# Attention and mixture-of-experts block on one Trainium2 core: the first scores in groups of four heads, POOL's normalisations as multiply and add, and unread matmuls ahead of the first scores

## The reference, cut to what matters

```python
def ref(x, ctx, lengths, ...):
    q = layernorm(x)                                   # (8, 128, 256): 8 heads of 16 channels, 256 queries
    s = 1 / (sqrt(64) * log(20)) * log(lengths)
    attn = softmax(s * einsum('bhdq,bhdk->bhqk', q, ctx))
    x = x + einsum('bhqk,bhdk->bhdq', attn, ctx)
    y = layernorm(x)
    # top-1 of eight experts with a capacity of 128 tokens each, plus a shared layer
    return x + gate * expert(y) + (silu(y @ sw1) * (y @ sw3)) @ sw2
```

## Time and profile before

| what | value |
|---|---|
| runs, median (lowest to highest) | 192.77 us (191.62 to 194.0), 3 runs |
| the profiled execution, its own time | 194.4 us |
| its span in the profile | 192.5 us |
| granted TensorE clock, mean | 0.949 |
| PE busy | 161.1 us (84%) |
| DVE, ACT, POOL busy | 104.3, 84.9, 70.9 us |

### The profile page before, as it was taken

One profiled execution on the slowest core, in us unless ns is written; L12 is line 12 of the kernel. 1 busy time (PEld: TensorE's weight loads), 2 busy tenths in 40 slices (PEclk: granted clock), 3 DMA queues, 4 the chain that ended last, 5 costly groups with the idle time before them and its releaser, 6 DMA issues.

```text
span 192.5 us, 3412 instructions
## 1 busy us (share of the span) xinstructions
PE 161.1 (84%) x1248; PEld 113.5 (59%) x1248; DVE 104.3 (54%) x236; ACT 84.9 (44%) x189; POOL 70.9 (37%) x79
## 2 busy tenths in 40 slices
PE   0399997999939999999999687299793999989960
PEld 0265566465425455555455387299692889878840
DVE  1466354556943778777341433422878228698630
ACT  2612122547453385665757363513761056455000
POOL 6644900691292081432202000044086047644241
PEclk9999999999985899999999999669999699999997
DMA  5999990000000000000070000002024935974001
GB/s 133 351 339 335 330 321 13 2 0 7 2 2 3 0 5 0 5 0 2 4 203 23 5 0 0 0 31 86 0 79 125 294 112 191 305 236 177 30 22 54
DMA packets 15697, 18.42 MB, mean 96 GB/s; under 512 B 1853, under 2 KB 14950, under 8 KB 15681
## 3 DMA queue, kind: packets, MB, share of 16 engines
q1 hardware_dynamic: 14240, 14.98, 25.3%
q0 software_dynamic: 1152, 2.97, 4.3%
q10 hardware_dynamic: 288, 0.26, 0.5%
HBM read 14.12 MB, written 4.21 MB: 95 GB/s over the span
## 4 chain that ended last, share of the span: by engine, by line
PE 70%; DVE 10%; DMA 5%; issue 5%; POOL 5%; ACT 2%; SPq 1%; DVEq 0%; POOLq 0%; ACTq 0%
PE bank L895 18%; PE bank L930 8%; PE bank L916 8%; PE bank L1049 5%; PE bank L977 5%; PE bank L979 4%; PE bank L1119 4%; DMA qz<-mrow 4%; POOL qz L352 3%; PE bank L1093 3%; PE bank L1094 3%; PE bank L942 2%; PE bank L957 2%; DMA leni<-in_lens 2%; PE bank L873 2%
## 5 line engine op out<-in xcount | busy, mean ns | idle before, releaser
L895 PE MATMUL bank<-kz,qz 32*128 32x256 f32 x256 | 50.2, 501 | 7.9 <-POOL qz L352 7.9
L487 DVE TENSOR_REDUCE nm<-bank 128x2 f32<-128x512 f32 x64 | 41.3, 686 | 26.7 <-PE bank L895 26.6
L916 PE MATMUL bank<-qz,kz 32*128 32x256 f32 x256 | 44.3, 442 | 1.1 <-DMA qz<-mrow 1.1
L733 ACT ACTIVATE pt<-bank 128x512 f32<-128x512 f32 x64 | 34.6, 590 | 23.1 <-PE bank L916 23.0
L895 PEld LDWEIGHTS bank<-kz,qz 32*128 32x128 f32 x256 | 31.2, 235 | 22.4 <-issue 16.1
L916 PEld LDWEIGHTS bank<-qz,kz 32*128 32x128 f32 x256 | 27.1, 205 | 6.5 <-issue 3.0
L352 POOL TENSOR_SCALAR qz<-xs,mv,rs 128x256 f32<-128x256 f32 x14 | 17.3, 1248 | 27.6 <-DVE rs L456 27.6
L930 PE MATMUL bank<-pt,vext 128*32 128x256 f32 x256 | 21.6, 413 | 0.0
L411 POOL DMA_INDIRECT expert_rows<-rk,idx_s x8 | 8.1, 1011 | 33.3 <-DVE rk L573 31.4
L377 POOL TENSOR_SCALAR rk<-xs,mv,rstd 128x256 f32<-128x256 f32 x6 | 7.4, 1225 | 31.9 <-ACT rstd L745 31.9
L434 POOL DMA_INDIRECT out<-vext,rk x8 | 8.3, 1037 | 13.1 <-DVE vext L652 9.1
(11 more groups left out here) (136 smaller groups left out, 302.4 us busy)
## 6 DMA issues: line engine op xcount, KB each, us to landing
wraw<-in_w SPq DMA_DIRECT2D x16, 352.0 KB, 7.2
wraw<-in_w SPq DMA_DIRECT2D x8, 256.0 KB, 7.1
expert_rows<-zero SPq DMA_DIRECT2D x1, 1032.0 KB, 10.3
out<-xs SPq DMA_DIRECT2D x8, 128.0 KB, 3.8
xs<-in_x SPq DMA_DIRECT2D x3, 256.0 KB, 4.3
cs<-in_ctx SPq DMA_DIRECT2D x3, 256.0 KB, 6.1
wraw<-in_w SPq DMA_DIRECT2D x8, 96.0 KB, 8.2
wraw<-in_sw SPq DMA_DIRECT2D x2, 352.0 KB, 5.6
```

The costliest lines, as they stand in the source:

```text
L487: nc.vector.tensor_reduce(nm[:, b % 2, :, place], mx_bank[n % NS][:].rearrange("p (u c) -> p u c", u=2), AX_X, ALU.max, negate=True).then_ ...
L733: nc.scalar.activation(pt[:, g % NPT, n % 4, :], sc_bank[n % NS][:], ACT.Exp).then_inc(exped, 1)
L895: mm = nc.tensor.matmul(mx_bank[n % NS][:, u * D:(u + 1) * D], qz[rows, b, half, u * P:(u + 1) * P], kz[rows, b, half, :], start=True, sto ...
L916: mm = nc.tensor.matmul(sc_bank[n % NS][:, c * D:(c + 1) * D], kz[rows, b, half, c * P:(c + 1) * P], qz[rows, b, half, :], start=True, sto ...
```

## The change

First scores: turns 0, 2, 4 and 6 issue the first scores of four heads (the last of two) at once, the first half of all four, then the second half. The first twelve heads (`FIRST`) go round six banks, head n waiting for the maximum of head n-6; the first three shifted scores wait for the maxima of heads 9, 10 and 11, whose banks they take. The transposed context now goes through bank 6 alone, one example at a time, in turns 1 to 8. POOL's queries become x * scale + (-mean * scale) with one more small DVE operation per chunk (`mrs`), POOL's token normalisation becomes x * rstd - (mean * rstd) with one more POOL operation on 128x1 (`mrs2`). PE's list begins with 50 rounds of four matmuls (bf16 ones, 32 rows by 128 columns, one in each row tile, into banks 0 to 3), which nobody reads.

```diff
+FIRST = 12
+IDLE_TURNS = 50
...
-VALUES = [min(b, LAG - 1) for b in range(B)]
+VALUES = [b + 1 for b in range(B)]
...
+            nc.gpsimd.memset(onesb[:], 1.0).then_inc(ones_set, 1)
             nc.gpsimd.memset(vext[:, :, :, :, HD:], 1.0).then_inc(ones_set, 1)
-            nc.gpsimd.memset(onesb[:], 1.0).then_inc(ones_set, 1)
...
-                pool.wait_ge(q_rs, chunk_of[b] + 1)
-                nc.gpsimd.tensor_scalar(qz[:, b, half, :], xs[:, b, :], mv[:, b, 0:1], rs[:, b, half:half + 1],
-                                        ALU.subtract, ALU.mult).then_inc(q_made, 1)
+                pool.wait_ge(q_shift, chunk_of[b] + 1)
+                nc.gpsimd.tensor_scalar(qz[:, b, half, :], xs[:, b, :], rs[:, b, half:half + 1],
+                                        mrs[:, b, half:half + 1], ALU.mult, ALU.add).then_inc(q_made, 1)
...
-                nc.gpsimd.tensor_scalar(x2[:, b, 0:D], xs[:, b, :], mv2[:, b, 0:1], rstd2[:, b:b + 1],
-                                        ALU.subtract, ALU.mult).then_inc(x2_made, 1)
+                nc.gpsimd.tensor_tensor(mrs2[:, b:b + 1], mv2[:, b, 0:1], rstd2[:, b:b + 1],
+                                        ALU.mult).then_inc(x_shift, 1)
+                pool.wait_ge(x_shift, b + 1)
+                nc.gpsimd.tensor_scalar(x2[:, b, 0:D], xs[:, b, :], rstd2[:, b:b + 1], mrs2[:, b:b + 1],
+                                        ALU.mult, ALU.subtract).then_inc(x2_made, 1)
...
+                dve.wait_ge(q_rs, i + 1)
+                nc.vector.scalar_tensor_tensor(mrs[:, a:z, :], mv[:, a:z, 0:1].broadcast_to(wide), -1.0,
+                                               rs[:, a:z, :], ALU.mult, ALU.mult).then_inc(q_shift, 1)
...
+                scores_bank = bank[n % (2 * NS) if n < FIRST else n % NS]
...
-                               sc_bank[b % NS][:, 0:2 * P].rearrange("p (c h d) -> p c h d", c=2,
+                               O[:, 0:2 * P].rearrange("p (c h d) -> p c h d", c=2,
...
+            def idle_turn(r):
+
+                nc.tensor.matmul(bank[r][:, 0:P], onesb[ROWS * r:ROWS * r + ROWS, :], onesb[ROWS * r:ROWS * r + ROWS, :],
+                                 start=True, stop=True)
+
+            pe.wait_ge(ones_set, 1)
+            for _ in range(IDLE_TURNS):
+                for r in range(4):
+                    idle_turn(r)
             pe.wait_ge(ld_cst, 16)
...
-                if b >= NS:
-                    pe.wait_ge(v_copied, b - NS + 1)
+                if b >= 1:
+                    pe.wait_ge(v_copied, b)
...
-                if n >= NS and u == 0:
-                    pe.wait_ge(maxed, n - NS + 1)
+                if n >= 2 * NS and u == 0:
+                    pe.wait_ge(maxed, n - 2 * NS + 1 if n < FIRST + NS else n - NS + 1)
...
-                if n == 0 and c == 0:
-                    pe.wait_ge(v_copied, B)
+                if n < NS and c == 0:
+                    pe.wait_ge(maxed, FIRST - NS + n + 1)
...
+                if m == 0:
+                    pe.wait_ge(v_copied, B)
...
+                if t < LAG and t % 2 == 0:
+                    heads = range(2 * t, min(2 * t + 4, 2 * LAG))
+                    for u in range(2):
+                        for n in heads:
+                            scores(n, u)
                 for part in range(2):
                     for k in range(2):
-                        if t < TURNS:
+                        if LAG <= t < TURNS:
                             scores(2 * t + k, part)
```

More of the change, by code:

```diff
@@ L163, in block_kernel @@
         rs = sb("rs", [P, B, 2], F32)
+        mrs = sb("mrs", [P, B, 2], F32)
         leni = sb("leni", [P, B], I32)
@@ L177, in block_kernel @@
         rstd2 = sb("rstd2", [P, B], F32)
+        mrs2 = sb("mrs2", [P, B], F32)
         x2 = rk
@@ L239, in block_kernel @@
         k_eager, k_made, q_eager, q_made = (sem(s) for s in ("k_eager", "k_made", "q_eager", "q_made"))
-        q_stats, q_mv, q_ln, q_rstd, q_rs = (sem(s) for s in ("q_stats", "q_mv", "q_ln", "q_rstd", "q_rs"))
+        q_stats, q_mv, q_ln, q_rstd, q_rs, q_shift = (
+            sem(s) for s in ("q_stats", "q_mv", "q_ln", "q_rstd", "q_rs", "q_shift"))
         v_turned, v_copied = sem("v_turned"), sem("v_copied")
@@ L246, in block_kernel @@
             sem(s) for s in ("o_copied", "o_turned", "inverted", "scaled", "o_back", "added"))
-        x_stats, x_mv, x_ln, x_rstd, x2_made = (sem(s) for s in ("x_stats", "x_mv", "x_ln", "x_rstd", "x2_made"))
+        x_stats, x_mv, x_ln, x_rstd, x_shift, x2_made = (
+            sem(s) for s in ("x_stats", "x_mv", "x_ln", "x_rstd", "x_shift", "x2_made"))
         x_turned, x_hi, x_lo = sem("x_turned"), sem("x_hi"), sem("x_lo")
@@ L486, in maximum @@
                 place = 4 * (h % 2) + h // 2
-                nc.vector.tensor_reduce(nm[:, b % 2, :, place], mx_bank[n % NS][:].rearrange("p (u c) -> p u c", u=2),
+                scores_bank = bank[n % (2 * NS) if n < FIRST else n % NS]
+                nc.vector.tensor_reduce(nm[:, b % 2, :, place], scores_bank[:].rearrange("p (u c) -> p u c", u=2),
                                         AX_X, ALU.max, negate=True).then_inc(maxed, 1)
@@ L710, in values @@
                 if b == 0:
-                    act.wait_ge(ones_set, 1)
+                    act.wait_ge(ones_set, 2)
                 nc.scalar.copy(vext[:, b, :, :, 0:HD],
-                               sc_bank[b % NS][:, 0:2 * P].rearrange("p (c h d) -> p c h d", c=2,
+                               O[:, 0:2 * P].rearrange("p (c h d) -> p c h d", c=2,
                                                                      h=H)).then_inc(v_copied, 1)
@@ L869, in turn_values @@
                 pe.wait_ge(ld_ctx[chunk_of[b]], 16)
-                if b >= NS:
-                    pe.wait_ge(v_copied, b - NS + 1)
+                if b >= 1:
+                    pe.wait_ge(v_copied, b)
                 for c in range(2):
-                    mm = nc.tensor.transpose(sc_bank[b % NS][:, c * P:(c + 1) * P], cs[:, b, c * P:(c + 1) * P], ident)
+                    mm = nc.tensor.transpose(O[:, c * P:(c + 1) * P], cs[:, b, c * P:(c + 1) * P], ident)
                 mm.then_inc(v_turned, 1)
@@ L892, in scores @@
                         pe.wait_ge(q_made, 2 * (b + 1) - EAGER)
-                if n >= NS and u == 0:
-                    pe.wait_ge(maxed, n - NS + 1)
-                mm = nc.tensor.matmul(mx_bank[n % NS][:, u * D:(u + 1) * D], qz[rows, b, half, u * P:(u + 1) * P],
+                if n >= 2 * NS and u == 0:
+                    pe.wait_ge(maxed, n - 2 * NS + 1 if n < FIRST + NS else n - NS + 1)
+                mm = nc.tensor.matmul(scores_bank[:, u * D:(u + 1) * D], qz[rows, b, half, u * P:(u + 1) * P],
                                       kz[rows, b, half, :], start=True, stop=True)
```

## The result

| | before | after |
|---|---|---|
| median of 20 runs each (lowest to highest) | 193.8 us (191.62 to 195.22) | 194.97 us (193.03 to 199.01) |
| ratio after / before, 95% interval | | 1.0097 (1.0065 to 1.0129) |
| the profiled execution: time, span | 194.4, 192.5 us | 194.63, 192.7 us |

The kernel became slower, by 1.2 us in the medians and by 1.9 us in the ratio, where 3.2 us of gain were forecast. It lies outside the stated range. The two profiled executions differ by 0.2 us only, because the one of before was 0.6 us slower than the median of its 20 runs.

A forecast was written before the change was run, and what follows sets the result against it. PE, busy 84% of the span, was taken as the bound, with waits on the maxima's transfer and POOL. Span: 192.5 + 0 + 2.2 - 5.4 = 189.3 us; from the median, -3.2 gives 189.6 us, range 186.2 to 193.4.

The forecast's parts named there:

- the moved values: Turns 7 to 9: transposes and ACT copies of examples 6 and 7 delay exponentials, +2.2 us, bounds 0 and 4.0.
- the clock behind 30 us: PE expected slow again after the pause, as before: gain and loss 0, bounds -1 and +1.5 us.
- rival (C): Clock rises later in turns 7 to 9 (+1.5), or the 57 us dip was not ordinary: 191.5 us, chance 0.18.
- Rival B: Moved values cost nothing, since exponentials have slack in turns 8 to 10: 187.4 us, chance 0.14.
- The transfer: Maxima's DMA before turn 7 stays behind weights and zeroing, landing unchanged at 30.0 us: gain 0, bounds 0 and 1.2.
- Rival A: The maxima's transfer follows its earlier issue, 1.2 to 4.8 us more gain, 3 taken: 186.6 us, chance 0.12.
- POOL: Around 51.6 us: multiply-and-add cuts PE's wait from 2.97 to 0.2 (2.8) and keeps the clock up (2.69), together 5.4 us.
- rival D: POOL's operation is not cheaper in the new form; the wait grows by 0.45 us: 195.4 us, chance 0.08.
- the token normalisation: On POOL, multiply then subtract, shown by no row, taken at 0.567 us, between 0.567 and 1.225.
- The rule that the operation should not matter: Trainium skill: bodies of at most two operations are port-bound at 1.03 cycles, so POOL's change would bring nothing.
- Unread matmuls: Kernel start: 50 rounds last 5 to 15.5 us, covered up to about 17; gain 0 and loss 0.
- rival E: Unread matmuls don't run side by side; 200 take 40 us and turn 7 is 24 us late: 214 us, chance 0.04.

The follow-up runs named there:

- e2: The kernel after without the unread matmuls at the start (IDLE_TURNS = 0): 193.99 us.
- e4: The kernel after with example 0's maxima DMAs issued by ACT right behind the row's copy, instead of by SP behind all loads: 187.07 us.
- e11: e3 plus the values moved through bank 6 in turns 1 to 8; first scores in pairs, no unread matmuls: 191.75 us.
- e1: The kernel after with the values of examples 6 and 7 made in turn 6 again: 190.71 us.
- e3: The kernel before with only POOL's queries as multiply and add, with the small DVE step: 188.47 us.
- e6: The kernel before with example 0's maxima DMAs issued by ACT instead of SP: 191.41 us, ratio 0.9944.
- e7: The kernel after with values in turn 6, token normalisation in one operation and example 0's maxima issued by ACT: 183.28 us.
- e8: e7 without the unread matmuls: 183.15 us.
- e10: e1 without unread matmuls and with token normalisation in one operation; that is e3 plus four heads in six banks: 189.06 us.
- e12: e1 with 45 rounds of unread matmuls in PE's pause between turns 6 and 7: 189.51 us.
- e13: The kernel after with ACT's copies of the values in turns 7 and 8 behind the turn's exponentials, PE untouched: 189.02 us.

## Why the prediction was wrong

**The step that failed is the moved values.** I took +2.2 us, with a bound of 4.0, and the clock behind 30 us at nothing, with a bound of +1.5. The direct part was nearly right: turns 7 to 9 took 2.45 us more. With the 1.44 us of the next stretch the term measured 3.9 us in the profiled pair, where the sum had 2.2. The copies came at 33.77 and 37.42, where I had put them. What I priced at nothing is what the hold-up does to the clock. With the copies ahead of the exponentials it rose 13.6 to 16.7 us after turn 7 (after, e2, e4, e11); without them 4.0 to 11.1 us (before, e1, e3, e6, e7, e8, e10, e12, e13). In the medians the move costs 3.3 us (e11 against e3) to 4.3 (e1 against after), by the ratios 2.4 to 5.0, and the mere order on ACT 5.9 (e13). That the part costs more than the whole is within the intervals. I had the mechanism, ACT's copy ahead of its exponentials, but named the clock as a separate rival (C) with 1.5 us, as another outcome in place of the forecast's; in the trace the two come together and add. Rival B, that the copies cost nothing, fell with them. That ACT's order costs the time is shown by e13, which changes nothing else. That the late clock follows from it rests on one trace of each kernel: four with the hold-up, nine without, and no overlap between them. Why the rise comes after 4.0 us in one and 11.1 in another, or 13.6 and 16.7, stays open.

**The transfer: right in its mechanism, off in size.** Rival A, a landing that comes earlier with an earlier issue, fell as long as SP issues. The front's gain was hidden completely, as said: e10 equals e3, and e4 sets it free. But I took the landing as unchanged. In six kernels with the faster front turn 7 began at 30.59 to 31.18, in before, e3 and e11 at 30.12 to 30.39. SP's first issue, started at 20.3 to 21.6 us, lasted 1.68 to 3.63 us in those six; started at 21.8 to 22.4 it lasted 0.66, 1.34 and 1.39 us in before, e11 and e3. Each landing was 6.8 to 7.9 us behind its end. In four of the six the earlier issue ended later than any of the three; in e2 and e13 it ended sooner (22.94 and 22.96 us), and the transfer took longer. I had also put the end of turn 6 before at 27 to 28 us; it was 29.00. A later landing I had not among my bounds (0 and 1.2 us of gain); it costs some 0.7 us, and why is not shown.

**POOL: right.** Forecast 5.4 us, measured 5.2 in the medians and 3.9 by the ratio (e3), so rival D fell. The queries took 565 ns (forecast 567), PE's wait fell to 0.57 (forecast 0.2), the dip is gone. The one miss is the token normalisation: multiply then subtract takes 1.23 us, no less than subtract then multiply, so the added product and its hand-over are a loss of 0.27 us (0.57 against 0.30). The small product was 0.189 us (0.20). The rule that the operation should not matter, which I weighed against the keys' row, does not hold here: the form with an add is twice as fast as both with a subtract. For the queries tile and shape stayed the same, and the operations and their scalar columns changed; the normalisation was never run with an add, so there the subtract is the likely cause and not a shown one.

**Unread matmuls: right.** 4.97 us for 50 rounds (rival E fell), and no worth that could be measured, in e2 or in e8.

**The sum again**, from medians: before 193.8; POOL's queries -5.2; faster front +0.6 (e10 against e3); moved values +3.3 to +4.3; the rest of e1 over e10, unread matmuls and the second POOL operation, +1.7. That is 194.2 to 195.2, against 194.97; the last two terms come from the same medians, so the agreement is in part by construction. By the ratios the terms are -3.9, +0.3, +5.0 and +0.5, together +1.9 us. The 1.7 is within the two intervals and I claim only 0.27 of it.

## What to carry to other kernels

When work is moved from a covered stretch into the critical one, look at what stands behind it in the list of each engine, not at its length: two copies of 0.37 us cost some 2 to 6 us because exponentials stood behind them, and putting them behind those in one list repaired it. Before a front stage is made faster, find the last thing the next stage waits for and who issues it; here 8 KB behind all loads hid the whole gain, and another engine's queue set it free. And measure the parts of a change one by one: here one part had all the gain of the change, and another gave most of it back.

## What the runs showed of the hardware that I had not expected

- POOL, float32, 128x256, two column scalars: multiply then add 0.565 us (queries after), subtract then multiply 1.25 (queries before), multiply then subtract 1.23 (normalisation after).
- A DMA issue of 4 KB on SP lasted up to 3.63 us (e10) behind the loads, whose own issues lasted up to 1.9 us (after, e1, e10), and the transfer landed 6.8 to 7.9 us after the issue ended.
- The granted clock in the profile stays at 1.00 until its first recorded change. Before showed 1.00 at 8 to 39 us while its matmuls took 629 ns; the kernel after showed 0.50 in turns 7 to 9 with the same 0.63 us. Only the durations tell the level there.
- 360 unread matmuls in a row, beside the loads, ran into holes of 3.04 and 1.49 us without a wait; the 200 at the start and 180 in the pause did not. The cause was not tested.
